# Layer 0 of an interaction network: the rest tile of the squares moved to the front, gathers at fixed steps, 36 extra products at the start

## The reference, cut to what matters

```python
e = stack([tbl_f[ids[:, f]] for f in range(39)], axis=1)     # 2048 x 39 x 16
x0 = xk = e
for W, b in ((w0, b0), (w1, b1), (w2, b2)):                  # 128 outputs each
    z = relu(einsum('bhd,bkd,hks->bsd', x0, xk, W) + b[None, :, None])
    # layers 0 and 1: xk = z[:, :64], the other 64 go to the output; layer 2: all 128
h = concatenate([sum over d of the outputs, dense_ctx], axis=1)   # 256 + 16
h = maximum(h @ W_top1 + b_top1, 0); h = maximum(h @ W_top2 + b_top2, 0)
y = h @ W_top3
```

## Time and profile before

| what | value |
|---|---|
| time, median of 3 runs | 2592.86 us (2591.3 to 2594.6) |
| the profiled execution, its own time | 2598.07 us |
| its span | 2596.2 us, granted clock 0.984 |
| PE busy | 2443.5 us (94%) |
| PE weight loads | 1591.3 us (61%) |
| DVE busy | 2169.6 us (84%) |
| ACT busy | 1661.3 us (64%) |
| POOL busy | 1875.1 us (72%) |
| hardware DMA queue | 61.6% of 16 engines' span |

### The profile page before, as it was taken

The page is one execution under the profiler, slowest core; times in us unless marked ns, Lnnn a source line. Parts: engine busy times, 40 slices in busy tenths (PEclk is TensorE's granted clock), DMA queues, the critical chain, the costliest instruction groups (busy, mean ns, idle before and its releaser), DMA issues.

```text
span 2596.2 us, 32413 instructions
## 1 busy us (share of the span) xinstructions
PE 2443.5 (94%) x8654; PEld 1591.3 (61%) x8654; DVE 2169.6 (84%) x1872; ACT 1661.3 (64%) x2120; POOL 1875.1 (72%) x1270
## 2 busy tenths in 40 slices
PE   0899999999999999999999999999999999999989
PEld 0466666666656666666666666666666666666655
DVE  1588889889878888988988898898888888888880
ACT  1566666666666666766666676666666666666653
POOL 6578778777867777777787777778777777765450
PEclk6899999999999999999999999999999999999999
DMA  2677667667757766766776676677667666756730
GB/s 71 139 149 155 126 138 166 134 131 151 154 110 152 154 130 132 166 137 132 148 158 129 132 164 140 127 150 155 131 131 166 141 131 145 160 129 129 159 80 0
DMA packets 214715, 352.58 MB, mean 136 GB/s; under 512 B 34382, under 2 KB 47566, under 8 KB 214588
## 3 DMA queue, kind: packets, MB, share of 16 engines
q1 hardware_dynamic: 194717, 347.07, 61.6%
q0 software_dynamic: 19968, 5.15, 2.2%
HBM read 346.97 MB, written 5.12 MB: 136 GB/s over the span
## 4 chain that ended last, share of the span: by engine, by line
POOL 30%; issue 27%; PE 16%; DVE 9%; DMA 7%; ACT 7%; SPq 3%; POOLq 0%; ACTq 0%; DVEq 0%; another core or an unknown queue 0%
POOL emb L374 13%; POOL Pl L380 13%; DMA xb<-x_dram 7%; ACT Ph L514 5%; PE ps L807 5%; PE ps L797 4%; DVE P L692 3%; DVE ps L692 3%; PE ps L817 3%; POOL dir L404 3%; SPq L311 3%; DVE Pl L697 3%; PE ps L926 1%; PE ps L918 1%; POOL emb L385 1%
## 5 line engine op out<-in xcount | busy, mean ns | idle before, releaser
L380 POOL TENSOR_TENSOR Pl<-P,Ph 128x1024 fp32r<-128x1024 f32 x448 | 1072.3, 2397 | 479.1 <-ACT Ph L514 469.4
L692 DVE TENSOR_TENSOR P<-xb,ps 128x1024 f32<-128x1024 f32 x768 | 926.8, 1214 | 81.1 <-DMA xb<-x_dram 72.9
L807 PE MATMUL ps<-Ph,wh 128*128 128x512 f32 x1920 | 870.1, 459 | 8.1 <-ACT Ph L514 8.0
L697 DVE TENSOR_TENSOR Pl<-ps,Ph 128x1024 fp32r<-128x1024 f32 x512 | 626.1, 1223 | 178.9 <-ACT Ph L514 168.7
L374 POOL DMA_INDIRECT emb<-tbl_in,idx x624 | 601.0, 963 | 166.3 <-issue 145.3
L807 PE MATMUL ps<-Ph,wl 128*128 128x512 f32 x1792 | 707.4, 395 | 0.0
L514 ACT ACTIVATE Ph<-ps 128x1024 fp32r<-128x1024 f32 x512 | 523.3, 1022 | 285.3 <-DVE ps L692 217.3
L817 PE MATMUL ps<-Pl,wh 128*128 128x512 f32 x1920 | 689.7, 445 | 11.4 <-POOL Pl L380 11.3
L514 ACT ACTIVATE Ph<-P 128x1024 fp32r<-128x1024 f32 x448 | 474.6, 1059 | 325.3 <-DVE P L692 303.8
L692 DVE TENSOR_TENSOR ps<-xb,ps 128x1024 f32<-128x1024 f32 x512 | 628.2, 1227 | 28.1 <-DMA xb<-x_dram 10.2
L797 PE MATMUL ps<-P,wp 128*128 128x512 f32 x1280 | 603.7, 594 | 4.1 <-DVE P L692 4.1
(11 more groups left out here) (64 smaller groups left out, 826.7 us busy)
## 6 DMA issues: line engine op xcount, KB each, us to landing
xb<-x_dram SPq DMA_DIRECT2D x1280, 256.0 KB, 8.5
emb<-tbl_in,idx POOLq DMA_INDIRECT x624
x_dram<-rows_sb SPq DMA_DIRECT2D x64, 78.0 KB
xb<-w_in SPq DMA_DIRECT2D x15, 128.0 KB
xb<-wt_in SPq DMA_DIRECT2D x2, 512.0 KB, 8.6
xb<-dense_in SPq DMA_DIRECT2D x1, 768.0 KB, 5.9
wp<-w_in SPq DMA_DIRECT2D x5, 128.0 KB
xb<-w0a_in SPq DMA_DIRECT2D x1, 448.0 KB
```

The costliest lines, as they stand in the source:

```text
L380: pool.tensor_tensor(Pl[:, h_slot(ref, c, k)], P[:, p_slot(ref, c, k)], Ph[:, h_slot(ref, c, k)], ALU.subtract).then_inc(low_pool, 1)
L692: dve.tensor_tensor(p, xb[:, x], xk.unsqueeze(1).broadcast_to([128, 2, N]), ALU.mult)\
L697: dve.tensor_tensor(Pl[:, h_slot(ref, c, k)], p_ps, Ph[:, h_slot(ref, c, k)], ALU.subtract)\
L807: pe.matmul(z_of(c, k), w[:, q, j, :], Ph[:, h_slot(ref, c, k), j, :], start=k in (L1B, L2) and i + j == 0, stop=False)
```

## The change

Four edits are made together.

1. **Order of layer 0's tiles.** Tile number 0 is now the rest; the six full tiles follow as 1 to 6. The rest's sum stands at PE step 2, its two squares at ACT step 5, `rest_low` at DVE step 6 of the same iteration, its contraction at PE step 9. The six full tiles are contracted at steps 8, 10, 12, 14, 16 and 18. The signal of `rest_low` has a semaphore of its own, `rest_ready`; the sum that follows the rest, at PE step 5, waits for it. `direct0`, `upper` and `lower` of layer 0 move from ACT steps 2, 3, 4 to 0, 1, 2, `direct2` from 5 to 4, and the full-precision copy of the embeddings from 15 to 17.
2. **Gathers.** The 39 gathers of a tile stand at steps given by a table, 9, 10, 11 and 9 in the four chunks of a tile (30 to 38 first, then 9, 12 and 9 before), and the indices for the tile after next are taken at chunk 1, step 18, and no longer at the start of chunk 2.
3. **The start.** Before the first transposes PE runs 36 products of 128 x 512 into z1, whose result nobody reads. The remainder of the first tile's embeddings is made by DVE and not by POOL. One more gather of the second tile comes early (13).
4. **The first chunk's layer 0** uses three banks: the two of `p_ps` beside `aux_ps`, so that three sums are issued at once.

```diff
+WARM = 36
-SUM_AT = [3, 5, 7, 9, 11, 13, 15]
-SQUARE_AT = [6, 7, 10, 12, 14, 16, 18]
-CONTRACT_AT = [6, 8, 10, 12, 14, 16, 19]
-REST_AT = 1
-DIRECT0_AT, UPPER0_AT, LOWER0_AT, RELU2_AT, DIRECT1_AT, RELU1_AT = 2, 3, 4, 5, 7, 8
-HIGH_AT, FULL_AT, LOW_AT = 15, 15, 17
+SUM_AT = [2, 5, 7, 9, 11, 13, 15]
+SQUARE_AT = [5, 7, 10, 12, 14, 16, 18]
+CONTRACT_AT = [9, 8, 10, 12, 14, 16, 18]
+REST_AT = 6
+DIRECT0_AT, UPPER0_AT, LOWER0_AT, RELU2_AT, DIRECT1_AT, RELU1_AT = 0, 1, 2, 4, 7, 8
+HIGH_AT, FULL_AT, LOW_AT = 15, 17, 17
-GATHER_AT = [k for k in range(STEPS) if KIND[k] != "G"]
+NEXT_IDS_AT = (1, 18)
+GATHERS = [[1, 2, 3, 5, 9, 14, 16, 17, 18], [1, 2, 3, 5, 6, 8, 9, 10, 18, 18],
+           [1, 2, 3, 5, 6, 9, 10, 12, 14, 16, 17], [1, 2, 3, 5, 6, 8, 9, 10, 17]]
+        early_ps = (ps[:, 6, :], ps[:, 7, :], aux_ps, ps[:, 7, :], aux_ps, ps[:, 7, :], aux_ps)
...
-            def rest_low(T, chunk):
+            def rest_low(T, chunk, bank=aux_ps):
                 dve.wait_ge(rest_square, T * CPT + chunk + 1)
-                dve.tensor_tensor(sqx[LAST_LO, :], aux_ps[LAST_LO], sqx[LAST_LO, :], ALU.subtract).then_inc(aux_read, 1)
+                dve.tensor_tensor(sqx[LAST_LO, :], bank[LAST_LO], sqx[LAST_LO, :], ALU.subtract).then_inc(rest_ready, 1)
...
-                        if k == REST_AT and not end and not (first and c == 0):
-                            rest_low(T, c + 1)
+                        if k == REST_AT and not (last and c >= 2):
+                            rest_low(T, c + 2)
...
+            for i in range(WARM):
+                pe.matmul(z1_ps[:, 0], wp[:, 0, 0, :], wp[:, 0:2].rearrange("p q j m -> p (q j m)"), start=True, stop=True)
...
+            transposes(0)
+            pe.wait_ge(aux_read, 1)
+            for t in range(3):
+                sums(t, early_ps[t])
+            for t in range(1, T0):
+                pe.wait_ge(aux_read, 1 + t)
+                contract0(t, 0, t == 1, False)
+                if t + 2 < T0:
+                    sums(t + 2, early_ps[t + 2])
+            pe.wait_ge(rest_ready, 1)
+            contract0(0, 0, False, True)
...
                         if k in SUM_AT and not no0:
                             t = SUM_AT.index(k)
-                            pe.wait_ge(aux_read, aux + 1 + t)
+                            if t == 1:
+                                pe.wait_ge(rest_ready, T * CPT + c + 3)
+                            else:
+                                pe.wait_ge(aux_read, aux + 1 + max(t - 1, 0))
                             sums(t)
```

More of the change, by code:

```diff
@@ L414, in _ @@
                 gather(f)
-            low_emb(0)
             def next_ids(T):
@@ L431, in tile @@
             def tile(T, ref, fields, first=False, last=False):
+                todo = [list(f) for f in fields]
                 for c in range(CPT):
[L434 to L437, removed]
                     for k in range(STEPS):
@@ L440, in tile @@
                             low(T, ref, c, k)
[L441 to L445, removed]
+                        if (c, k) == NEXT_IDS_AT and todo[2]:
+                            next_ids(T + 2)
+                        part = min(c, 1) if (c, k) < NEXT_IDS_AT else 2
+                        n = GATHERS[c].count(k) * (1 + (first and c == 0))
+                        for f in todo[part][:n]:
+                            gather(f)
+                        todo[part] = todo[part][n:]
                         if c == 0 and not first and k in FOLD1_AT:
@@ L463, in tile @@
                             low_emb(T + 1)
-            cuts = (0, 12, 21, 30, NF)
-            third, fourth, first, second = (range(a, b) for a, b in zip(cuts, cuts[1:]))
-            tile(0, 0, (range(early, 30), range(30, NF), third, fourth), first=True)
+            late, soon = len(GATHERS[0]), len([k for k in GATHERS[1] if (1, k) < NEXT_IDS_AT])
+            cut = NF - late - soon
+            assert sum(map(len, GATHERS)) == NF
+            start, middle, rest = range(0, cut), range(cut, cut + late), range(cut + late, NF)
+            tile(0, 0, (range(early, cut + late), rest, start), first=True)
             with pool.Fori(1, TILES - 2) as T:
-                tile(T, 1, (first, second, third, fourth))
-            tile(TILES - 2, TILES - 2, (first, second, (), ()))
-            tile(TILES - 1, TILES - 1, ((), (), (), ()), last=True)
+                tile(T, 1, (middle, rest, start))
+            tile(TILES - 2, TILES - 2, (middle, rest, ()))
+            tile(TILES - 1, TILES - 1, ((), (), ()), last=True)
             pool.wait_ge(z2_read, chunks)
@@ L537, in _ @@
                 copy_x(0, AUX * g)
-                for t in range(T0):
-                    square(0, AUX * g + 1 + t, t)
+                if g:
+                    rest_squares(0, AUX * g + 1)
+                for t in range(1, T0):
+                    square(0, AUX * g + 1 + t, t - 1, aux_ps if g else early_ps[t])
+                    if t == 1 and not g:
+                        rest_squares(0, 1, early_ps[0])
                     s = t - (T0 - PRE - 1)
@@ L708, in _ @@
             for s in range(PRE):
+                if s == 1:
+                    rest_low(0, 1)
                 dve.wait_ge(xb_in[s], 32)
@@ L851, in _ @@
             late = None
[L852 to L865 removed]
+            transposes(0)
+            pe.wait_ge(aux_read, 1)
+            for t in range(3):
+                sums(t, early_ps[t])
+            for t in range(1, T0):
+                pe.wait_ge(aux_read, 1 + t)
[4 more added lines that the diff above has]
+            contract0(0, 0, False, True)
+            transposes(1)
+            for t in range(T0):
+                if t == 1:
+                    pe.wait_ge(rest_ready, 2)
+                else:
+                    pe.wait_ge(aux_read, READS + 1 + max(t - 1, 0))
+                sums(t)
+                if t:
+                    if t > 1:
+                        pe.wait_ge(aux_read, READS + t)
+                    contract0(t - 1, 1, t == 1, False)
+                if t >= T0 - PRE:
+                    late = contract(0, 0, -1, L1B + t - (T0 - PRE), late)
+            pe.wait_ge(aux_read, 2 * READS)
+            contract0(T0 - 1, 1, False, True)
             assert not late
```

75 lines of the change are left out of this document (37 added, 38 removed).

## The result

| | before | after |
|---|---|---|
| time, median | 2592.3 us (2591.3 to 2594.6) | 2667.96 us (2667.6 to 2668.8) |
| ratio to before, 95% interval | | 1.0291 [1.0273, 1.0309] |
| profiled execution, its span | 2598.07, 2596.2 us | 2667.91, 2666.1 us |
| PE, DVE busy | 2443.5, 2169.6 us | 2500.3, 2177.7 us |
| ACT, POOL busy | 1661.3, 1875.1 us | 1654.5, 1868.2 us |

The changed kernel is 2.9% slower. The median before now has four runs and not three. In the changed kernel the product is L706, the remainder L711, `rest_low` L717, the sum L800, the full contraction L805, the rest's contraction L807, the high part L827, the low part L837, the plain step L817, the rounding L521, `direct0` L530 and `direct1` L533.

What follows compares the result with a forecast made beforehand. The prediction took a ring through PE, ACT's `direct0` and DVE to bound the changed kernel at 39.08 us a chunk: +71.4 over 61 intervals, +5.5 stalls, together +77, -3 start, so +74 and 2667 us; range 2612 to 2692.

Steps and rivals of the forecast that it cites:

- The ring through `direct0`: PE's step 5 sum through step 18, ACT's `direct0` and roundings, DVE's `rest_low`, back to the sum: longest, 39.08 us a chunk.
- The ring of the DMAs: DVE step 10, broadcasts, step 4, `rest_low`, PE's sum, `direct1`: 38.4 us a chunk; as only bound 2625 us, chance 0.20.
- The wait at the sum: PE's step 5 sum waits for DVE's `rest_low` in nearly every chunk, about 1.5 us each, some 90 us in all.
- the 6.74: Forecast time in us on PE from the sum of step 5 to the high part of step 8.
- PE's own work: PE's time per chunk without its wait for `rest_low` at the rest's contraction: 36.83 us.
- Single stalls: Stalls elsewhere in the run, 10.9 us in the kernel before; half kept, +5.5 us, bounds 0 and 10.9.
- The start: Transposes 1.2 us earlier by DVE's remainder, first chunk's layer 0 1.8 us shorter by three banks: -3.0 us.
- The bound of -7: Largest gain allowed at the start, including up to 4 us if the 36 products ended right at the first transposes.
- Gathers and indices: New steps for POOL's gathers and indices: 0 expected, at most -10 us, up to +10 us.
- The full prize: Rival: the wait at the rest's contraction goes and nothing takes its place, -55 - 3, 2535 us; chance 0.06.
- the trade of waits: Rival: PE's sum waits 0.78 us where the rest's contraction waited 0.89, 2583 us; chance 0.08.
- the half clock: Rival: the 36 start products run at half clock, end at 84.4 us, transposes 22 us late, 2689 us; chance 0.04.

Runs made afterwards that it cites:

- e7: Changed kernel with only the broadcast pairs issued in the order 0, 1, 4 to 9, 2, 3: ratio to before 1.0271, chunk 39.10 us.
- e1: Changed kernel with layer 0's `direct0`, `upper` and `lower` back at ACT steps 2, 3, 4: 2646.96 us, ratio to before 1.0178.
- e8: Changed kernel with `direct0` back at ACT step 2 and the broadcast pairs reordered: 2568.51 us, ratio to before 0.9889.
- e2: Kernel before with only `rest_low` moved one step forward, to DVE step 0: 2562.95 us, ratio 0.9867.
- e12: Kernel before with only the broadcast pairs reordered to 0, 1, 4 to 9, 2, 3: 2584.55 us, ratio 0.9951.
- e9: Kernel before with `rest_low` at step 0 and the broadcast pairs reordered: 2533.12 us, ratio 0.9750.
- e10: Changed kernel with 44 extra products at the start in place of 36: 2671.38 us, ratio to before 1.0289.
- e4: Changed kernel with gathers and indices at nearly their old steps: ratio to before 1.0311, chunk 39.22 us.

## Why the prediction was right, point by point

**The sign and the main step held.** Forecast was 2667 us, measured 2667.96. The profiled executions are the fairer test: +74 forecast, 2667.91 - 2598.07 = +69.8 measured, made of +73.3 in the 61 intervals and -3.4 outside them, which is what the first chunk gained. That the medians agree to 1 us is partly luck: the profiled execution before stood 5.2 us above its median, the one after on it.

**The ring through `direct0`: right, term by term**, 39.10 us against 39.08, no term off by more than 0.15 (table above). The largest, 19.94 against 19.79, is in part the rest's single pass: it was put at 0.34 us, read behind a wait, and takes 0.23 without one (1176.69 to 1176.92). That the ring is the one that binds is shown by experiments: without broadcast waits nothing changes (e7), and with it opened the chunk falls to what the DMAs allow (e1).

**The ring of the DMAs: right.** Forecast 38.4 and ranked as a rival, it is measured at 38.6 to 38.75 as soon as `direct0` is back (e1), and removed it gives 1.3 us a chunk more (e8). It was also there in the kernel before, covered: it took back part of the prize of e2. But the prediction says that the waits for broadcasts cost nothing in the kernel before, and that isn't quite so: without them it is 0.5% faster (e12), as one of them stood ahead of `rest_low`.

**The wait at the sum: the place right, the size too large.** Forecast about 1.5 us each and some 90 in all; measured 65.2 us in 61 cases, 1.07 each. The rest stands at the high part of step 7, 0.69 us behind its rounding, which I had not named. The prediction saw that one contraction fewer stands there and that PE gains nothing by it, but not that the gain turns into a second wait: just this contraction had covered `direct1` and the rounding of step 7 on ACT. How the 1.5 us came out of its sums it doesn't say. The sum of the ring was not touched, since it passes that place by way of ACT (the 6.74), but e8 is held there: with both rings opened it needs 37.49 us where e9 needs 36.91.

**PE's own work: 0.2 us too large.** 36.83 us was a chunk less its listed wait; e9 runs at 36.63 (median). The list leaves out a part of each wait (see the last section). So the prize of a kernel without waits was about 1.2 us a chunk and not 0.89, of which e9 got 1.0. The forecast did not rest on it, as the ring is longer than either; but the 10.9 us kept for single stalls held this error too.

**Single stalls: oversized.** I kept +5.5 us for them; the mean of the intervals (39.11) and their median (39.10) show under 1 us over the run.

**The start: right within 0.4 us.** `direct0` of the first chunk came at 75.52 us instead of 78.94, 3.4 us earlier against 3.0. DVE made the remainder in 1.26 us and the transposes started at 62.20. The products cost nothing and gave nothing: from 22.61 they took 31.70 us, 0.88 us each, and ended at 54.3, and the granted clock then fell, as the stretches of the changed kernel show:

```profile
54.00:56.00 2.00, 0.31 (x1) 0.00 (x0) 0.00 (x0) 0.00 (x0) 1.69 (x2) 1.00 0.08 8
56.00:58.00 2.00, 0.00 (x0) 0.00 (x0) 0.00 (x0) 0.00 (x0) 1.39 (x3) 0.96 0.05 4
58.00:60.00 2.00, 0.00 (x0) 0.00 (x0) 0.00 (x0) 0.00 (x0) 0.57 (x1) 0.50 0.09 8
```

The bound of -7, in which up to 4 us stood for products that end right at the transposes, was too generous by about 3 (e10).

**Gathers and indices: 0 forecast, none measurable** (e4).

**The rivals.** The full prize and the trade of waits are excluded by the chunk of 39.11 us and the 65.2 us at L800, the ring of the DMAs as the only bound by e7, the half clock by the 0.88 us for each product.

What stays open is how far the changed order would come if the bubble at step 7 were filled too (e8 stands at 37.49 us a chunk, e9 at 36.91): a kernel with `direct0` back, the broadcasts reordered and a contraction at step 6 was not tried. Nor were the three banks of the first chunk, the place of `direct2` or that of the full-precision copy of the embeddings varied alone.

## What to carry to other kernels

A wait of 0.9 us on the busiest engine is not a prize until the loops that run through several engines have been added up: walk each ring once around (engine to engine, back to the same instruction one iteration later) and write its length beside the busiest engine's own work. Moving a signal earlier pays only if what then waits for it, and all that queues behind that waiter, has slack; here moving one subtraction by one step gained 1.3%, and moving the whole chain to another place lost 2.9%. Where two rings are nearly of one length, opening one shows almost nothing, so try them in pairs before an edit is called useless.
